# Attention: the product with V in fp32 in four column groups of 32

## The chip, the cores and the metric

The kernel runs on one core of one Trainium2 chip. The metric is the device time of an execution in microseconds. Its engines are TensorE (PE, with its weight loads as PEld), VectorE (DVE), ScalarE (ACT), GpSimd (POOL) and SyncE (SP, which here only starts DMAs). The matmul array can be used in parts: a matmul whose weights have 64 or fewer columns takes a column group, and two that use different groups can be on their way together.

## The reference

The program is one layer over 4096 tokens of width 256: a linear attention, a layer norm, then a transformer block (softmax attention with 16 heads of 16, and a mixture of 8 experts), and a last layer norm. The change touches the softmax attention alone:

```
h = _layernorm(x, ln1_g, ln1_b)
q = (h @ Wq).reshape(Bb, Ss, H, Dh)
k = (h @ Wk).reshape(Bb, Ss, H, Dh)
v = (h @ Wv).reshape(Bb, Ss, H, Dh)
scores = jnp.einsum('bqhd,bkhd->bhqk', q, k) / jnp.sqrt(jnp.float32(Dh))
attn = jax.nn.softmax(scores, axis=-1)
ctx = jnp.einsum('bhqk,bkhd->bqhd', attn, v).reshape(Bb, Ss, Dd)
```

Here Bb is 1, Ss is 4096, H is 16 and Dh is 16. All is fp32.

## The kernel before

The function `softmax_attention` goes through 128 chunks: 16 heads, each with 8 chunks of 512 queries. The 4096 keys stand on two sides of 2048, one in array rows 0 to 49 and one in rows 64 to 113, so that two score matmuls run beside each other. A chunk has 16 units t, each of 128 keys of either side. Each engine has its own program, and semaphores tie them together; the order on PE is written out by hand:

- In each slot t of a chunk PE computes the scores S of unit t (`scores`, two matmuls, line 701) into one of two banks `s_ps`, and ACT turns them into `probs` with Exp (line 790).
- Two chunks ahead (LEAD), PE computes the same products the other way round in pairs, M (`max_pair`, line 693), into three banks `m_ps` that take turns. DVE reduces each to a maximum over 512 keys (line 824, 683 ns). For the units in RELU_PAIRS, the first M holds a difference of two sides' keys, ACT takes its relu (line 777) and one DVE operation (line 818) adds the second M to it and reduces both at once. The next M into a bank waits (`m_read`, `excess_ready`) until the bank was read.
- In the slots of SLOTS, PE adds probabilities times V to `o_ps` (`values`, one or two units in a visit). Slots of 16 and more fall into the next chunk. Slot 9 and slot 11 have no visit.
- In slot 8 ACT copies `o_ps` to `o_here`, in slot 11 PE adds up its pieces through the matrix `gather` (`turn_o`, line 735), DVE copies the result to `ctx_stage` (line 832), and SP stores it.
- DVE's `finish_max` takes the maximum of a chunk in slot 0 and transposes it in slot 6 (line 842). Between the two POOL splits it in two parts (`split_max`, lines 628 to 631). SP writes it with 16 small DMAs (`rows`, line 545) as two more rows of the queries. PE waits for these before the chunk.

For 11 of the 16 units the product with V is split: the upper half of each fp32 probability read as bf16 and the rest of it as f16 (`probs_low`, which POOL computes, line 640), both against V in three bf16 pieces, 49 of 64 columns (line 726). The five FULL_UNITS take fp32 probabilities against fp32 V (line 720); these visits stand in slots 12, 15, 18, 21 and 24, that is in slots 12, 15, 2, 5 and 8 of a chunk. The last column of V is ones, which gives the sum of the probabilities. At the start of a head POOL splits V anew (`split_v`, lines 609 to 620).

Of the kernel before, what the change touches and what calls it, by code (L numbers as in the profile page):

```python
# [465 lines left out]
def softmax_attention(nc, dram, keep):  # L466

    with ExitStack() as ctx:
# [53 lines left out]
        def _(sp):  # L522
# [36 lines left out]
            def chunk(h, qc, loads=True, more=True, ahead=True, before=True):  # L559

                i = sp.snap(h * CHUNKS + qc)
                if loads:
                    sp.wait_ge(s_done, i * UNITS + 1)
                    n = qc + LEAD + 1
                    load_q(sp.snap(h + n // CHUNKS), n % CHUNKS, n % Q_BUFS)
                    if more and qc == 0:
                        load_head(sp.snap(h + 1), sp.snap((h + 1) & 1))
                if ahead:
                    rows(i + 1, (qc + 1) % Q_BUFS)
                if before:  # L570
# [14 lines left out]
        def _(pool):
            ch = Chain(pool, v_chain)
            nc.gpsimd.memset(k_ring[:, :, :].bitcast(F32), 1.0).then_inc(ones_set, 1)  # L587
            nc.gpsimd.memset(v_parts[:, :, :, V_ONE:V_COLS], 0.0).then_inc(v_consts, 1)
            nc.gpsimd.memset(v_full[:, :, :, :, :], 0.0).then_inc(v_consts, 1)
            nc.gpsimd.memset(zeros[:, :, :], 0.0).then_inc(v_consts, 1)  # L590
            nc.gpsimd.memset(gather[:, :], 0.0).then_inc(v_consts, 1)
            pool.wait_ge(v_consts, 4)
            nc.gpsimd.memset(v_parts[:, :, :, V_ONE:V_ONE + 1], 1.0).then_inc(v_consts, 1)
            nc.gpsimd.memset(v_full[:, :, :, :, V_ONE:V_ONE + 1], 1.0).then_inc(v_consts, 1)
            starts = [k * V_COLS + DH * n for k in range(2) for n in range(PIECES)]
            nc.gpsimd.tensor_tensor(gather[:, 0:DH], ident[:, 0:DH], ident[:, DH:2 * DH], ALU.add).then_inc(gather_chain, 1)
            for n, r in enumerate(starts[2:]):
                pool.wait_ge(gather_chain, n + 1)
                nc.gpsimd.tensor_tensor(gather[:, 0:DH], gather[:, 0:DH], ident[:, r:r + DH], ALU.add).then_inc(gather_chain, 1)
            nc.gpsimd.tensor_tensor(gather[:, DH:O_COLS], ident[:, V_ONE:V_ONE + 1],  # L600
                                    ident[:, V_COLS + V_ONE:V_COLS + V_ONE + 1], ALU.add).then_inc(gather_chain, 1)
            pool.wait_ge(gather_chain, len(starts))
            pool.wait_ge(v_consts, 6)
            pool.sem_inc(gather_ready, 1)

            def split_v(h, par):

                high, mid, low = (v_parts[:, par, :, DH * n:DH * n + DH] for n in range(PIECES))
                ch.inc(nc.gpsimd.tensor_copy(v_here[:, :, :], v_all[:, :, ds(h * DH, DH)]))
                ch.wait()  # L610
                for n, t in enumerate(FULL_UNITS):
                    at = first_tile(t)
                    ch.inc(nc.gpsimd.tensor_tensor(v_full[:, par, n, :, 0:DH], v_here[:, at:at + 3:2, :], zeros[:, 0:2, :], ALU.add))
                ch.inc(nc.gpsimd.tensor_tensor(high, v_here[:, :, :], zeros[:, :, :], ALU.add))
                ch.wait()
                ch.inc(nc.gpsimd.tensor_tensor(v_rest[:, :, :], v_here[:, :, :], high, ALU.subtract))
                ch.wait()
                ch.inc(nc.gpsimd.tensor_tensor(mid, v_rest[:, :, :], zeros[:, :, :], ALU.add))
                ch.wait()
                ch.inc(nc.gpsimd.tensor_tensor(low, v_rest[:, :, :], mid, ALU.subtract))  # L620
                ch.wait()
                pool.sem_inc(v_ready, 1)
# [11 lines left out]
            def split_probs(i, more=True):  # L634

                for t in POOL_UNITS:
                    if more and t == POOL_UNITS[MAX_PLACE]:
                        split_max(i + 1)
                    pool.wait_ge(exp_done, i * UNITS + (t + 1))
                    nc.gpsimd.tensor_tensor(probs_low[:, LOW_UNITS.index(t), :, :], probs[:, t, :, :],  # L640
                                            high_view[:, t, :, :, 1], ALU.subtract).then_inc(pool_low_done, 1)

            def split_chunks(lo, hi):
# [12 lines left out]
            split_chunks(0, CHUNKS + 1)  # L656
            with pool.Fori(0, HEADS // 2 - 1) as pair:
                ch.enter(pair, 2 * SPLIT_OPS)
                for par in range(2):
# [11 lines left out]
        def _(pe):
# [33 lines left out]
            def values(it, c, visit):  # L705
# [6 lines left out]
                for t in VISITS[visit]:  # L712
                    if t in POOL_UNITS:
                        pe.wait_ge(pool_low_done, i * len(POOL_UNITS) + (POOL_UNITS.index(t) + 1))
                    if t in DVE_UNITS:
                        pe.wait_ge(dve_low_done, i * (2 * len(DVE_UNITS)) + 2 * (DVE_UNITS.index(t) + 1))
                    first, final = t == VISITS[0][0], t == VISITS[-1][-1]
                    if t in FULL_UNITS:
                        for k in range(2):
                            last = nc.tensor.matmul(o_ps[V_COLS * k:V_COLS * k + V_COLS, :],  # L720
                                                    v_full[:, par, FULL_UNITS.index(t), k, :], probs[:, t, k, :],
                                                    start=False, stop=final)
                        continue
                    for n, part in enumerate((high_view[:, t, :, :, 1], probs_low[:, LOW_UNITS.index(t), :, :])):
                        for k in range(2):
                            last = nc.tensor.matmul(o_ps[V_COLS * k:V_COLS * k + V_COLS, :],  # L726
                                                    v_parts[:, par, first_tile(t) + 2 * k, :], part[:, k, :],
                                                    start=(first and n == 0), stop=(final and n == 1))
                last.then_inc(pv_done, 1)

            def turn_o(it, c):
# [3 lines left out]
                nc.tensor.matmul(m_ps[:, TURN_BLOCK % 3, :], gather[:, :], o_here[:, :], start=True, stop=True  # L735
                                 ).then_inc(o_turned, 1)
# [999 lines left out]
```

## Time and profile before

| what | us |
|---|---|
| median of 3 runs | 4357.15 |
| lowest and highest | 4355.73, 4363.25 |
| the profiled execution | 4349.05 |
| its span, first to last instruction | 4347.1 |
| attention's chunks in the span | about 357 to 3468 |
| PE, POOL, ACT, DVE busy | 3934.0, 3413.5, 2829.4, 2750.1 |
| mean granted clock of TensorE | 0.931 of full |

The page says how long each engine was busy. It does not say what waited for what: for that one reads the timeline of one chunk, engine by engine, and compares the start of an instruction with the end of what it needs. The records of one fp32 matmul are two, since it goes through the array in two passes; "x4" on line 720 stands for two matmuls.

### The profile page before, as it was taken

The page shows a single profiled execution, that of the slowest core. Times are in us where ns is not written, and L with a number is a line of the kernel's source. Part 1 is how long each engine was busy: PE and PEld are TensorE (multiplying, and loading weights), DVE is VectorE, ACT ScalarE, POOL GpSimd, SP SyncE. Part 2 cuts the span into 40 slices and gives each one's busy share as a digit, 9 for nine tenths or more (in the row PEclk, how much of TensorE's full clock was granted, in tenths as well). Part 3 has the DMA queues.
Part 4 walks back from the last instruction along what each step waited for, and adds up shares of the span by engine and source line. Part 5 has one row for each costly group of instructions (what it writes and reads, how often), then busy time and mean ns, then how long its engine had stood idle before and what let it go on. Part 6 is the DMA issues. An engine that isn't in the chain of part 4 may idle for free. (4 is left out here: it accounts for less than half of the span.)

```text
span 4347.1 us, 74722 instructions
## 1 busy us (share of the span) xinstructions
PE 3934.0 (90%) x21172; PEld 1901.6 (44%) x21172; DVE 2750.1 (63%) x5522; ACT 2829.4 (65%) x3421; POOL 3413.5 (79%) x2261
## 2 busy tenths in 40 slices
PE   7469999999999999999999999999999970999990
PEld 4234333333333333333333333333333360899990
DVE  2537777777777777777777777777777451333335
ACT  2125878777787878777787878777788710555550
POOL 0015898989888898988888898988988826888865
PEclk8677999999999999999999999999999975999995
DMA  2241011010101011010101011010100053443434
GB/s 86 111 137 19 11 21 22 10 22 10 22 10 22 10 22 21 11 21 10 22 10 22 10 22 21 11 21 12 20 11 10 17 186 109 140 144 132 147 101 121
DMA packets 145717, 205.12 MB, mean 47 GB/s; under 512 B 43536, under 2 KB 108432, under 8 KB 140176
## 3 DMA queue, kind: packets, MB, share of 16 engines
q1 hardware_dynamic: 127072, 173.76, 14.9%
q0 software_dynamic: 6336, 16.79, 1.2%
q10 hardware_dynamic: 12144, 12.06, 0.8%
q8 instruction: 141, 2.31, 0.2%
q14 instruction: 24, 0.20, 0.0%
HBM read 134.59 MB, written 66.85 MB: 46 GB/s over the span
## 5 line engine op out<-in xcount | busy, mean ns | idle before, releaser
L640 POOL TENSOR_TENSOR probs_low<-probs 128x1024 f16<-128x1024 f32 x1408 | 2632.3, 1894 | 331.0 <-ACT probs L790 324.6
L790 ACT ACTIVATE probs<-s_ps 128x1024 f32<-128x1024 f32 x2048 | 2081.7, 1026 | 240.3 <-PE s_ps L701 190.5
L824 DVE TENSOR_REDUCE unit_max<-m_ps 128x1 f32<-128x512 f32 x2816 | 1779.0, 683 | 222.4 <-PE m_ps L693 181.7
L701 PE MATMUL s_ps<-q_stage,k_ring 50*128 50x512 f32 x4096 | 1043.0, 504 | 1.2 <-DMA q_stage<-max_turned 0.9
L693 PE MATMUL m_ps<-k_ring,q_stage 48*128 48x512 f32 x3456 | 959.5, 424 | 64.3 <-DMA q_stage<-qs_dram 25.4
L701 PEld LDWEIGHTS s_ps<-q_stage,k_ring 50*128 50x128 f32 x4096 | 388.5, 186 | 1160.0 <-issue 907.8
L818 DVE CUSTOM_DVE_ANT_0 excess<-m_ps,excess 128x512 f32<-128x512 f32 x640 | 442.8, 692 | 550.5 <-ACT excess L777 543.9
L720 PE MATMUL o_ps<-probs,v_full 128*64 128x512 f32 x2560 | 698.0, 624 | 0.0
L777 ACT ACTIVATE excess<-m_ps 128x512 f32<-128x512 f32 x640 | 382.1, 597 | 449.8 <-PE m_ps L693 449.8
L726 PE MATMUL o_ps<-probs,v_parts 128*64 128x512 bf16 x2816 | 586.3, 413 | 0.9 <-POOL probs_low L640 0.7
L693 PEld LDWEIGHTS m_ps<-k_ring,q_stage 48*128 48x128 f32 x3456 | 514.8, 192 | 160.5 <-DVE unit_max L824 113.8
L726 PE MATMUL o_ps<-probs_low,v_parts 128*64 128x512 f16 x2816 | 543.2, 383 | 0.0
L1565 DVE TENSOR_TENSOR hidden_low<-h_ps,hidden_high 128x512 fp32r<-128x512 f32 x184 | 127.3, 692 | 365.7 <-ACT hidden_high L1529 365.7
L726 PEld LDWEIGHTS o_ps<-probs,v_parts 128*64 128x64 bf16 x2816 | 156.1, 108 | 379.0 <-issue 304.2
L1525 ACT ACTIVATE h_ps<-h_ps,b_here 128x512 f32<-128x512 f32 x184 | 121.3, 659 | 255.1 <-PE h_ps L1462 255.0
L693 PE MATMUL m_ps<-kd_ring,q_stage 48*128 48x512 f32 x640 | 258.3, 404 | 1.2 <-DVE unit_max L824 1.2
L587 POOL MEMSET k_ring<- 114x4096 f32 x1 | 3.5, 3516 | 293.0 <-POOLq L114 293.0
L1474 PE MATMUL y_ps<-w_low,hidden_high 128*128 128x256 f32 x736 | 209.0, 284 | 0.0
L1474 PE MATMUL y_ps<-w_high,hidden_high 128*128 128x256 f32 x736 | 207.4, 282 | 0.0
L1474 PE MATMUL y_ps<-w_high,hidden_low 128*128 128x256 f32 x736 | 206.6, 281 | 0.0
L720 PEld LDWEIGHTS o_ps<-probs,v_full 128*64 128x64 f32 x2560 | 127.6, 135 | 174.2 <-issue 173.6
L1421 POOL TENSOR_TENSOR w_high<-w_in,zero 128x1024 fp32r<-128x1024 f32 x44 | 130.5, 2983 | 68.3 <-PEq L1493 60.8
(198 smaller groups left out, 3586.6 us busy)
## 6 DMA issues: line engine op xcount, KB each, us to landing
w_in<-in_W SPq DMA_DIRECT2D x46, 1024.0 KB, 4.9
q_stage<-max_turned SPq DMA_DIRECT2D x2048, 0.5 KB
q_stage<-qs_dram SPq DMA_DIRECT2D x768, 32.0 KB, 1.8
k_ring<-ks_dram SPq DMA_DIRECT2D x96, 128.0 KB, 4.2
slots_dram<-zero_rows SPq DMA_DIRECT2D x24, 512.0 KB, 6.3
rows_e<-slots_dram SPq DMA_DIRECT2D x24, 512.0 KB, 3.9
y_slots_dram<-y_out ACTq DMA_DIRECT2D x23, 512.0 KB, 4.3
qs_dram<-parts SPq DMA_DIRECT2D x16, 512.0 KB, 2.8
```

Source lines behind the costliest of these rows:

```text
L640: nc.gpsimd.tensor_tensor(probs_low[:, LOW_UNITS.index(t), :, :], probs[:, t, :, :], high_view[:, t, :, :, 1], ALU.subtract).then_inc(pool ...
L693: nc.tensor.matmul(m_ps[:, b % 3, :], q_stage[at:at + SROWS, col:col + P], ring[at:at + SROWS, par, key:key + CHUNK], start=True, stop=Tru ...
L701: last = nc.tensor.matmul(s_ps[:, t % 2, k, :], k_ring[at:at + AROWS, par, P * t:P * t + P], q_stage[at:at + AROWS, buf * CHUNK:buf * CHUN ...
L720: last = nc.tensor.matmul(o_ps[V_COLS * k:V_COLS * k + V_COLS, :], v_full[:, par, FULL_UNITS.index(t), k, :], probs[:, t, k, :], start=Fal ...
L726: last = nc.tensor.matmul(o_ps[V_COLS * k:V_COLS * k + V_COLS, :], v_parts[:, par, first_tile(t) + 2 * k, :], part[:, k, :], start=(first ...
L777: nc.scalar.activation(excess[:, :], m_ps[:, block_of(t, 0) % 3, :], ACT.Relu).then_inc(excess_ready, 1)
L790: nc.scalar.activation(probs[:, t, :, :], s_ps[:, t % 2, :, :], ACT.Exp).then_inc(exp_done, 1)
L818: nc.vector.tensor_tensor_reduce(excess[:, :], m_ps[:, block_of(t, 1) % 3, :], excess[:, :], 1.0, LEAST, ALU.add, ALU.max, unit_max[:, b, ...
L824: nc.vector.tensor_reduce(unit_max[:, b, qt, 2 * j + k:2 * j + k + 1], m_ps[:, block_of(t, k) % 3, :], AX.X, ALU.max).then_inc(m_read, 1 + ...
L1421: nc.gpsimd.tensor_tensor(w1_high[:, b, half, :, :], w1[:, half, :, :], zero[:, :].unsqueeze(2).to_broadcast([P, FT, P]), ALU.add).then_in ...
L1474: last = nc.tensor.matmul(y_ps[:, b, t // 2, D * (t % 2):D * (t % 2) + D], h[:, f % 4, cols], w[:, b, f, :], start=(f == 0 and n == 0 and ...
L1565: nc.vector.tensor_tensor(hidden_low[:, f % 4, :], h_ps[:, f % 2, :], hidden_high[:, f % 4, :].bitcast(F32), ALU.subtract).then_inc(low_do ...
```

## The change

All 16 units now take fp32 probabilities against fp32 V. `probs_low`, the three pieces of V and all that POOL did for them are gone; POOL copies a head's V (`copy_v`) and splits the maxima. V has 32 columns for each key tile (16 values, a column of ones, zeros). A visit takes two units with their two sides, four matmuls in four column groups of 32, over half of the queries: a visit of all 512 queries in slot 10 for units 0 and 1, then 14 visits of 256 queries in slots 11 to 24. Only slot 9 has none. `turn_o` becomes four matmuls of 128 queries side by side, so that `ctx_stage` has 128 partitions by 128, and its store takes five DMAs in place of two. The relu units go from five (2, 5, 8, 12, 15) to four (2, 5, 11, 14), the transpose of the maxima from slot 6 to slot 2. Any M whose bank was last read by a relu now waits for ACT's signal. SP starts a head's K loads after the rows, not ahead of them.

```diff
-VISITS = ((0, 1), (3,), (2,), (4,), (6,), (5,), (7,), (9,), (8,), (10,), (12,), (11,), (13, 14), (15,))
-SLOTS = (10, 12, 13, 14, 15, 16, 17, 18, 19, 20, 21, 22, 23, 24)
+VISITS = ((0, 0, CHUNK),) + tuple((p, lo, lo + HALF) for p in range(1, UNITS // 2) for lo in (0, HALF))
+SLOTS = tuple(range(10, 25))
-RELU_PAIRS = (2, 5, 8, 12, 15)
-FINISH_SLOTS = (0, 6)
+RELU_PAIRS = (2, 5, 11, 14)
+FINISH_SLOTS = (0, 2)
...
-                    if more and qc == 0:
-                        load_head(sp.snap(h + 1), sp.snap((h + 1) & 1))
                 if ahead:
                     rows(i + 1, (qc + 1) % Q_BUFS)
+                if more and qc == 0:
+                    load_head(sp.snap(h + 1), sp.snap((h + 1) & 1))
...
+            def copy_v(h, par):
+
+                ch.inc(nc.gpsimd.tensor_copy(v_here[:, par, :, 0:DH], v_all[:, :, ds(h * DH, DH)]))
                 ch.wait()
                 pool.sem_inc(v_ready, 1)
...
-                    if k == 1 and (t - 1) % UNITS in RELU_PAIRS and t - 1 != TURN_SLOT and c * UNITS + t > 0:
+                    past = [r for r in RELU_PAIRS if block_of(r, 0) in (b - 3, b - 3 + RING_BLOCKS)]
+                    if past and c * RING_BLOCKS + b > 2:
...
+                pair, lo, hi = VISITS[visit]
+                for t in (2 * pair, 2 * pair + 1):
+                    for k in range(2):
+                        at = SQ * (2 * (t % 2) + k)
+                        last = nc.tensor.matmul(o_ps[at:at + SQ, lo:hi], v_here[:, par, first_tile(t) + 2 * k, :],
+                                                probs[:, t, k, lo:hi], start=(pair == 0), stop=(pair == UNITS // 2 - 1),
+                                                skip_group_check=True)
                 last.then_inc(pv_done, 1)
...
-                nc.tensor.matmul(m_ps[:, TURN_BLOCK % 3, :], gather[:, :], o_here[:, :], start=True, stop=True
-                                 ).then_inc(o_turned, 1)
+                for t in range(TPC):
+                    last = nc.tensor.matmul(m_ps[SQ * t:SQ * t + SQ, TURN_BLOCK % 3, 0:P], gather[:, :],
+                                            o_here[:, P * t:P * t + P], start=True, stop=True)
+                last.then_inc(o_turned, 1)
```

On PE, slots 2 and 3 and the start of slot 4 of a chunk, before (line 701 is S, 693 is M, 720 and 726 are V):

```order
L701 MATMUL s_ps<-q_stage,k_ring 128x512 [waits exp_done]
L701 MATMUL s_ps<-q_stage,k_ring 128x512
L693 MATMUL m_ps<-kd_ring,q_stage 128x512 [waits m_read]
L693 MATMUL m_ps<-k_ring,q_stage 128x512 [waits m_read]
L720 MATMUL o_ps<-probs,v_full 64x512 x2
L701 MATMUL s_ps<-q_stage,k_ring 128x512 [waits exp_done]
L701 MATMUL s_ps<-q_stage,k_ring 128x512
L693 MATMUL m_ps<-k_ring,q_stage 128x512 [waits m_read]
L693 MATMUL m_ps<-k_ring,q_stage 128x512 [waits excess_ready]
L726 MATMUL o_ps<-probs,v_parts 64x512 [waits pool_low_done]
L726 MATMUL o_ps<-probs,v_parts 64x512
L726 MATMUL o_ps<-probs_low,v_parts 64x512 x2
```

and in the changed kernel (line 661 is S, 653 is M, 676 is V):

```order
L661 MATMUL s_ps<-q_stage,k_ring 128x512 [waits exp_done]
L661 MATMUL s_ps<-q_stage,k_ring 128x512
L653 MATMUL m_ps<-kd_ring,q_stage 128x512 [waits m_read]
L653 MATMUL m_ps<-k_ring,q_stage 128x512 [waits m_read]
L676 MATMUL o_ps<-probs,v_here 32x256 x4
L661 MATMUL s_ps<-q_stage,k_ring 128x512 [waits exp_done]
L661 MATMUL s_ps<-q_stage,k_ring 128x512
L653 MATMUL m_ps<-k_ring,q_stage 128x512 [waits m_read]
L653 MATMUL m_ps<-k_ring,q_stage 128x512 [waits excess_ready]
L676 MATMUL o_ps<-probs,v_here 32x256 x4
L661 MATMUL s_ps<-q_stage,k_ring 128x512 [waits exp_done]
L661 MATMUL s_ps<-q_stage,k_ring 128x512
```

Behind the M pair of relu unit 2, two full matmuls of 512 queries have become four of 256, and the split visit of slot 3 another four.

On PE, slots 10 and 11, before:

```order
L701 MATMUL s_ps<-q_stage,k_ring 128x512 [waits exp_done]
L701 MATMUL s_ps<-q_stage,k_ring 128x512
L693 MATMUL m_ps<-k_ring,q_stage 128x512 [waits m_read] x2
L726 MATMUL o_ps<-probs,v_parts 64x512 [waits pool_low_done,o_copied]
L726 MATMUL o_ps<-probs,v_parts 64x512
L726 MATMUL o_ps<-probs_low,v_parts 64x512 x2
L726 MATMUL o_ps<-probs,v_parts 64x512 [waits pool_low_done]
L726 MATMUL o_ps<-probs,v_parts 64x512
L726 MATMUL o_ps<-probs_low,v_parts 64x512 x2
L701 MATMUL s_ps<-q_stage,k_ring 128x512 [waits exp_done]
L701 MATMUL s_ps<-q_stage,k_ring 128x512
L693 MATMUL m_ps<-k_ring,q_stage 128x512 [waits m_read] x2
```

and now, from S of slot 10 (line 686 is `turn_o`):

```order
L661 MATMUL s_ps<-q_stage,k_ring 128x512 [waits exp_done]
L661 MATMUL s_ps<-q_stage,k_ring 128x512
L653 MATMUL m_ps<-k_ring,q_stage 128x512 [waits m_read] x2
L676 MATMUL o_ps<-probs,v_here 32x512 [waits o_copied]
L676 MATMUL o_ps<-probs,v_here 32x512 x3
L661 MATMUL s_ps<-q_stage,k_ring 128x512 [waits exp_done]
L661 MATMUL s_ps<-q_stage,k_ring 128x512
L653 MATMUL m_ps<-kd_ring,q_stage 128x512 [waits m_read]
L653 MATMUL m_ps<-k_ring,q_stage 128x512 [waits m_read]
L676 MATMUL o_ps<-probs,v_here 32x256 x4
L686 MATMUL m_ps<-o_here,gather 32x128 [waits m_read,o_copied]
L686 MATMUL m_ps<-o_here,gather 32x128 x3
```

Slot 10 keeps a long visit, now of one pair of units; slot 11 has become a relu slot with a visit ahead of `turn_o`, which is four matmuls of 128 queries.

On SP, a head's first chunk, before (line 535 loads queries, 526 and 529 the next head's K, 545 writes rows):

```order
L535 DMA q_stage<-qs_dram 16x512 [waits s_done]
L535 DMA q_stage<-qs_dram 16x512 x5
L526 DMA k_ring<-ks_dram 16x2048 x6
L529 DMA kd_ring<-kd_dram 16x2048 x3
L545 DMA q_stage<-max_turned 1x4x32 [waits max_ready]
L545 DMA q_stage<-max_turned 1x4x32 x15
L535 DMA q_stage<-qs_dram 16x512 [waits s_done]
```

and now (518, 509 and 512, 528):

```order
L518 DMA q_stage<-qs_dram 16x512 [waits s_done]
L518 DMA q_stage<-qs_dram 16x512 x5
L528 DMA q_stage<-max_turned 1x4x32 [waits max_ready]
L528 DMA q_stage<-max_turned 1x4x32 x15
L509 DMA k_ring<-ks_dram 16x2048 x6
L512 DMA kd_ring<-kd_dram 16x2048 x3
L518 DMA q_stage<-qs_dram 16x512 [waits s_done]
```

The rows of the next chunk no longer stand behind the nine K loads.

## Rows read from the trace of the kernel before

**Rows 1.** The page: busy time of each engine over the span.

```profile
PE 3934.0 (90%) x21172; PEld 1901.6 (44%) x21172; DVE 2750.1 (63%) x5522; ACT 2829.4 (65%) x3421; POOL 3413.5 (79%) x2261
```

**Rows 2.** Busy time by stretch: us, engines with (instructions), PEclk, DMA share, GB/s.

```profile
400.00:3440.00 3040.00, 3003.02 (x16256) 1173.45 (x16252) 2250.82 (x4356) 2392.53 (x2752) 2721.79 (x1893) 0.98 0.09 16
769.00:798.00 29.00, 27.36 (x138) 10.56 (x134) 18.78 (x38) 19.93 (x24) 28.10 (x25) 0.88 0.04 9
```

**Rows 3.** Timeline, SyncE, 1400 to 1610 us: start, us, engine, line, operation.

```profile
1408.75 2.69 SPq L535 DMA_DIRECT2D q_stage<-qs_dram  x6
...
1551.06 2.69 SPq L535 DMA_DIRECT2D q_stage<-qs_dram  x6
...
1579.36 2.69 SPq L535 DMA_DIRECT2D q_stage<-qs_dram  x6
```

**Rows 4.** The same for PE, 1500 to 1526 us, one chunk's slots 6 to 12.

```profile
1511.33 0.50 PE L701 MATMUL s_ps<-q_stage,k_ring 50*128 50x512 f32 x2
...
1512.00 0.41 PE L726 MATMUL o_ps<-probs,v_parts 128*64 128x512 bf16 x2
...
1512.56 0.50 PE L701 MATMUL s_ps<-q_stage,k_ring 50*128 50x512 f32 x2
...
1514.62 0.40 PE L693 MATMUL m_ps<-kd_ring,q_stage 48*128 48x512 f32 x1
...
1514.94 1.08 PE L720 MATMUL o_ps<-probs,v_full 128*64 128x512 f32 x4
1515.95 0.50 PE L701 MATMUL s_ps<-q_stage,k_ring 50*128 50x512 f32 x2
1516.29 0.40 PE L693 MATMUL m_ps<-k_ring,q_stage 48*128 48x512 f32 x2
1516.62 0.49 PE L701 MATMUL s_ps<-q_stage,k_ring 50*128 50x512 f32 x2
1516.95 1.02 PE L693 MATMUL m_ps<-k_ring,q_stage 48*128 48x512 f32 x2
1517.90 0.42 PE L726 MATMUL o_ps<-probs,v_parts 128*64 128x512 bf16 x2
...
1519.57 1.13 PE L735 MATMUL m_ps<-o_here,gather 128*128 128x512 f32 x2
1520.63 0.50 PE L701 MATMUL s_ps<-q_stage,k_ring 50*128 50x512 f32 x2
```

**Rows 5.** The same for PE's weight loads, 1517 to 1518 us.

```profile
1517.47 0.18 PEld L693 LDWEIGHTS m_ps<-k_ring,q_stage 48*128 48x128 f32 x1 [0.56 <-DVE unit_max L824]
```

**Rows 6.** The same for ACT.

```profile
1515.05 0.60 ACT L777 ACTIVATE excess<-m_ps 128x512 f32<-128x512 f32 x1 [0.85 <-PE m_ps L693]
```

**Rows 7.** The same for DVE.

```profile
1513.31 0.23 DVE L842 STREAM_TRANSPOSE max_turned<-max_parts 128x64 f32<-128x64 f32 x1
1513.47 1.25 DVE L824 TENSOR_REDUCE unit_max<-m_ps 128x1 f32<-128x512 f32 x2
1515.92 0.69 DVE L818 CUSTOM_DVE_ANT_0 excess<-m_ps,excess 128x512 f32<-128x512 f32 x1 [1.20 <-ACT excess L777]
...
1516.73 2.48 DVE L824 TENSOR_REDUCE unit_max<-m_ps 128x1 f32<-128x512 f32 x4
```

**Rows 8.** All engines at the start of a head, 769 to 785 us.

```profile
769.74 0.61 POOL L609 COPY v_here<-v_all 128x512 f32 x1
...
781.37 0.24 DVE L842 STREAM_TRANSPOSE max_turned<-max_parts 128x64 f32<-128x64 f32 x1 [2.38 <-POOL max_parts L631]
```

**Rows 9.** SyncE in a head's first chunk.

```profile
1333.06 3.00 SPq L526 DMA_DIRECT2D k_ring<-ks_dram  x6
1336.26 1.34 SPq L529 DMA_DIRECT2D kd_ring<-kd_dram  x3
1339.94 9.87 SPq L545 DMA_DIRECT2D q_stage<-max_turned  x16
```

**Rows 10.** Busy time of line 1116 alone, the densest stretch of loads and matmuls.

```profile
3535.40:3537.00 1.60, 1.60 (x15) 1.60 (x16) 1.00 1.04 339
```

More of the change, by code:

```diff
@@ L84, in visit_of @@
 def visit_of(t):
-    return [t in units for units in VISITS].index(True)
+    return max(n for n, (pair, lo, hi) in enumerate(VISITS) if pair == t // 2)
 class Chain:
@@ L593, in _ @@
[L593 to L603, printed above, removed]
-            pool.sem_inc(gather_ready, 1)
[L606 to L620, printed above, removed]
@@ new lines, in _ @@
+            pool.wait_ge(v_consts, 2)
+            nc.gpsimd.memset(v_here[:, :, :, DH:O_COLS], 1.0).then_inc(v_consts, 1)
+            nc.gpsimd.tensor_tensor(gather[:, 0:O_COLS], ident[:, 0:O_COLS], ident[:, SQ:SQ + O_COLS], ALU.add
+                                    ).then_inc(gather_chain, 1)
+            for n in range(2, P // SQ):
+                pool.wait_ge(gather_chain, n - 1)
+                nc.gpsimd.tensor_tensor(gather[:, 0:O_COLS], gather[:, 0:O_COLS], ident[:, SQ * n:SQ * n + O_COLS], ALU.add
+                                        ).then_inc(gather_chain, 1)
@@ L632, in split_max, with split_maxima @@
                                         ).then_inc(max_split, 1)
[L634 to L643, printed above, removed]
+            def split_maxima(lo, hi):
                 with pool.Fori(lo, hi) as i:
-                    split_probs(i)
+                    split_max(i + 1)
             for h in range(2):
-                split_v(h, h)
+                copy_v(h, h)
             pool.wait_ge(unit_set, 3)
@@ L655, in _ @@
                                     ).then_inc(max_split, 1)
-            split_chunks(0, CHUNKS + 1)
+            split_maxima(0, CHUNKS + 1)
             with pool.Fori(0, HEADS // 2 - 1) as pair:
-                ch.enter(pair, 2 * SPLIT_OPS)
+                ch.enter(pair, 2)
                 for par in range(2):
@@ L711, in values @@
                     pe.wait_ge(v_ready, it * 2 + (c // CHUNKS + 1))
[L712 to L728, printed above, removed]
+                pair, lo, hi = VISITS[visit]
[5 more added lines that the diff above has]
+                                                skip_group_check=True)
                 last.then_inc(pv_done, 1)
@@ L843, in finish_max, with chunk @@
                                         max_parts[:, :, :].bitcast(F32).rearrange("p r n -> p (r n)")).then_inc(max_ready, 1)
-            def low(i, t, k):
-                dve.wait_ge(exp_done, i * UNITS + (t + 1))
-                nc.vector.tensor_tensor(probs_low[:, LOW_UNITS.index(t), k, :], probs[:, t, k, :], high_view[:, t, k, :, 1],
-                                        ALU.subtract).then_inc(dve_low_done, 1)
-            def chunk(n, b, ahead=True, finish=True, turn=True, stores=None, current=True):
+            def chunk(n, b, ahead=True, finish=True, turn=True, stores=None):
                 for t in range(UNITS):
@@ L863, in chunk @@
                             dve.sem_inc(m_read, RING_BLOCKS - 1 - TURN_BLOCK)
-                    if current and t in DVE_PLACES:
-                        low(n - LEAD, *DVE_PLACES[t])
                     if finish and not ahead and t == FINISH_SLOTS[0]:
@@ L869, in chunk @@
                         finish_max(n - 1, 1 - b, FINISH_SLOTS.index(t))
-            chunk(0, 0, finish=False, turn=False, current=False)
-            chunk(1, 1, turn=False, current=False)
+            chunk(0, 0, finish=False, turn=False)
+            chunk(1, 1, turn=False)
             chunk(2, 0, turn=False)
@@ L881, in _ @@
             chunk(RING + 1, 1, ahead=False, finish=False, stores=RING // 2 - 1)
-            chunk(RING + 2, 0, ahead=False, finish=False, stores=RING // 2 - 1, current=False)
+            chunk(RING + 2, 0, ahead=False, finish=False, stores=RING // 2 - 1)
 def row_statistics(nc, dve, ch, stats, mean_var, std, rstd, var_ready, std_ready, n):
```

53 lines of the change are left out of this document (18 added, 35 removed).

## The prediction

> **What bounds the kernel now.** I read the page first, then the busy time by stretch. Over the span PE is busy 90%, POOL 79%, ACT 65%, DVE 63% [rows 1]. In the attention stage, 400 to 3440 us, PE is busy 3003 of 3040 us, POOL 2722, and the granted clock is 0.98, so nearly all of it at the upper of the two levels, 2.4 GHz [rows 2]. The reader is to see that the stage is 70% of the span and that PE has no room in it; the other stages are untouched by the diff and stay as they are.
>
> Next, the period of a chunk from SyncE's query loads: six chunks start between 1408.75 and 1551.06, 23.72 us each, and the seventh, the second of a head, takes 28.30 [rows 3]. There are 128 chunks and 14 such long ones, 4.58 us each above the others.
>
> Then one chunk on PE in order of time [rows 4]. A slot is a score pair S, a maximum pair M, and mostly a visit of the values, V. S to M is 0.34 us (1515.95 to 1516.29), M to what follows 0.33 (1516.29 to 1516.62). A split unit (bf16 and f16) takes 0.56 (1512.00 to 1512.56), a full fp32 unit 1.01 (1514.94 to 1515.95), turn_o 1.06 (1519.57 to 1520.63). Added up for a chunk: 16 x 0.67 + 11 x 0.50 (four of the split units stand in two visits of about 1.0, so 7 x 0.56 + 2 x 1.0 = 5.9) + 5 x 1.01 + 1.06 = 22.7 us. The other 1.0 us of 23.72 is waiting, and one place holds most of it: at slot 10 the second M waits from 1516.95 to 1517.47 and V starts at 1517.90 in place of 1517.28, 0.62 late [rows 4, 5].
>
> Last, why it waits, since the change rearranges just that. A relu unit runs PE, ACT, DVE in series: M starts at 1514.62, relu at 1515.05, the DVE operation at 1515.92, the next reduce at 1516.73, and the M two units later goes at 1517.47, when that reduce has freed its bank [rows 4 to 7]. So from M to relu 0.43, to DVE 0.87, to the next reduce 0.81, to the freed bank 0.74: 2.85 us. PE needs two slots for that way, and where they are shorter it waits. Before, a full unit of 1.01 us stands behind the M of each relu unit, and only the empty slot 9 is too short.
>
> **The change part by part.**
>
> *Values.* 54 matmuls in 14 visits become 60 in 15: one of 512 queries, 14 of 256, each with four matmuls in four column groups. The trace has only two groups at once. Full minus split unit is 1.01 - 0.56 = 0.45 us; both have two groups, and the full one streams twice as long, so 0.43 to 0.45 us is what half the columns of a full visit take. If four groups stream beside each other as two do, a half visit takes 1.01 - 0.43 = 0.58 us and holds two units. Bounds: 0.56 (a split visit, which streams as long), and 1.01 if the groups go two by two. I take 0.58, the nearest row. The sum is 14 x 0.58 + 1.01 = 9.1 us a chunk against 10.9.
>
> *turn_o.* One fp32 matmul of 512 columns becomes four of 128 side by side: about 0.4 us in place of 1.06 (a quarter of the 0.86 that streams, and the 0.2 around it). Its output on DVE shrinks too. Neither ends up on the path, see the walk.
>
> PE without any wait would then need 16 x 0.67 + 9.1 + 0.4 = 20.3 us a chunk, 2.4 less than the 22.7 of before. That would be 2.4 x 127 = 305 us plus the saved waits. I do not take it, because the slots behind relu units are now 1.25 us each (0.34 + 0.33 + 0.58), 2.5 for two, and the way across ACT and DVE takes 2.85 and its wait breaks up an M pair.
>
> *The walk of one chunk, with relu at units 2, 5, 11, 14.* Times from S of slot 2.
> - Relu 2: M 0.34, relu 0.77, DVE 1.64, free 2.45, the transpose that now stands here 0.16 (1513.31 to 1513.47) [rows 7], reduce of unit 3 at 2.61, bank free 3.35. M of unit 4 would have been at 2.84, so it waits 0.5. A lone second M takes 0.43 to V (1517.47 to 1517.90). V 0.58, S of slot 5 at 4.36. The banks that a relu frees are now waited for by ACT's own signal, which comes before DVE's and is on time.
> - Relu 5: 2.45 + 0.74 + 0.43 + 0.58 = 4.20, S of slot 8 at 8.56; slot 8 nothing special, S of slot 9 at 9.81.
> - Slot 9 is empty: its reduce starts 0.77 after S, bank free 1.51, then 0.43, and V of 512 queries 1.01: S of slot 11 at 12.76.
> - Relu 11: M of unit 12 waits for the DVE operation itself, free at 2.37; + 0.43 + 0.58: S of slot 13 at 16.14. turn_o (0.4) ends before that wait does and costs nothing.
> - Slot 13 1.25, relu 14 4.20: S of slot 1 at 21.59, slot 1 1.25, S of slot 2 at 22.84.
>
> So the period is 22.84 us, not 20.3: DVE and the relu way become the bound and PE waits 2.5 us a chunk. The gain is 23.72 - 22.84 = 0.88 us x 127 = 112 us. A V that is off by 0.05 counts seven times on this path, 0.35 us.
>
> *POOL.* It loses all low parts (79% busy falls to a few per cent). They cost PE little in an ordinary chunk, but at a head's start the split of V (from 769.74) holds POOL up and DVE waits 2.38 us for the maxima behind it at 781.37, PE behind DVE; the clock there averages 0.88 [rows 2, 8]. What remains is one copy of V, 0.61 us. So the 14 long chunks become ordinary: 14 x 4.58 = 64 us. What is late next there is SyncE: nothing of PE waits for the K loads until the next head.
>
> *SyncE.* In a head's first chunk: query loads 2.7, rows 9.87, K loads 3.00 + 1.34, and five stores in place of two, about 2.5: 19.4 us against 22.8 [rows 3, 9]. The rows now go ahead of the K loads: they start behind the transpose of slot 2, about 5 us into the chunk, and are all issued by about 15. Cost nothing; if the cover is gone, 1 to 4 us in 15 chunks. The wait of a store holds only the next query loads, which are wanted two chunks later.
>
> *Rest.* relu 4 for 5, with two more reduces, is in the walk. The end of the stage has no POOL wait and shorter visits, but three more stores: about -1.
>
> Sum against the profiled execution's 4349 us: 4349 - 112 - 64 - 1 = 4172. The median of the runs, 4357, is 8 us above that execution; I forecast 4174.
>
> **The rivals.**
>
> 1. *Column groups two by two.* A half visit takes 1.01, the long one 1.87, turn_o 0.7: 10.7 + 14.1 + 1.9 + 0.7 = 27.4, with a wait left at slot 10 about 27.6 us. (27.6 - 23.72) x 127 = +493, - 64: 4777. It decides from a half visit of 0.78 on: the period is then 22.84 + 7 x 0.20 = 24.2, whose loss of 0.5 us a chunk eats the heads' 64 us. For it: no row shows more than two groups, and four read four different fp32 streams at once. Against: the two that run now show no slowing by each other. 0.11.
> 2. *Four groups at once but dearer*, 0.65 to 0.75 a half visit, by the streams or by issue. A load with its matmul comes every 0.107 us at the densest [rows 10]; a slot now has 12 such pairs, 1.28 us against its 1.25. At 0.70: 22.84 + 7 x 0.12 = 23.7, only the heads' 64 us are gained: 4285. 0.08. The Trainium skill ("TensorE: Matmul & The Clock Gate", section Measured speedup) gives 2.38x for three column tiles and 3.07x for four row tiles, not 3 and 4. By an estimate from 3.07 of 4 a half visit would be 0.71 and the time that of this rival; no run here shows four groups.
> 3. *PE does not wait*: the way across ACT and DVE overlaps better than my walk has it, period 21.5 or less: 4349 - 282 - 65 = 4000. Against: the 0.62 at slot 10 comes out of the same steps. 0.05.
> 4. *The clock.* PE's idle share grows from about 4% to 11%. After the 2.4 us wait at a head's start it fell [rows 2, 8]; the longest wait of the walk is 0.5. If chunks ran at 1.2 GHz, S, M and V double: over 30 us a chunk, above 5000. 0.03.
>
> **How the numbers follow.** The walk has 0.73, with a range of its own of 22.2 to 23.4 us a chunk, 4090 to 4245. The range is 4085 to 4265: it adds the mild end of rival 2 and leaves out 0.11 for rival 1, 0.03 for the clock, and about 0.07 beyond the rest. What a measurement of this kernel can tell from no change is 0.2%, 9 us. Faster: 0.73 + 0.05 + most of rival 2 = 0.84. Same 0.03. Slower 0.13, rivals 1 and 4 with one case of rival 2 beyond the even point.
>
> **What would show it.** From one half visit's start to the next S: 0.58 (right), 0.7 (rival 2), 1.01 (rival 1). Query loads 22.8 us apart, the head's second chunk like the others. Second M of units 4, 7, 10, 12 and 0 waiting for DVE 0.3 to 0.5 us each, and the relu way still 0.43, 0.87, 0.81, 0.74. No POOL wait, clock 0.98 or more. Wrong would be: PE full at 20.3 us, waits at other units, or a wait of DVE for rows or stores.

## The result, and the profile after

The changed kernel takes 4080.6 us (median of 4 runs, 4078.6 to 4083.5), the kernel before on the same chip 4356.4 us (4353.6 to 4363.3): a ratio of 0.9365, 95% interval 0.9349 to 0.9381. It is 276 us faster; the forecast was 182 us faster, 4174 us, with a range from 4085 to 4265. The measured time lies 4 us below that range.

The page of the changed kernel, busy time of each engine over its span of 4078.9 us, beside [rows 1]:

```profile
PE 3651.7 (90%) x29108; PEld 1882.1 (46%) x29108; DVE 2718.8 (67%) x5522; ACT 2680.2 (66%) x3293; POOL 696.5 (17%) x703
```

and the attention stage by stretch, the columns those of [rows 2]:

```profile
400.00:3200.00 2800.00, 2745.12 (x24272) 1161.52 (x24264) 2220.80 (x4357) 2267.46 (x2655) 77.07 (x389) 1.00 0.10 18
```

POOL has lost its work, PE stays at the same share of a shorter stage, and the granted clock is 1.00, the upper level, 2.4 GHz. SyncE's query loads from a head's first chunk on stand beside [rows 3]; they are 22.10, 21.53 and 22.15 us apart:

```profile
1248.93 2.70 SPq L518 DMA_DIRECT2D q_stage<-qs_dram  x6
...
1271.03 2.70 SPq L518 DMA_DIRECT2D q_stage<-qs_dram  x6
...
1292.56 2.70 SPq L518 DMA_DIRECT2D q_stage<-qs_dram  x6
...
1314.71 2.70 SPq L518 DMA_DIRECT2D q_stage<-qs_dram  x6
```

There is no chunk of 28 us any more. Measured from one chunk's first exponential to the next one's, the median period is 23.72 us before and 22.15 us after. So the time went like this in the two profiled executions, which are 268 us apart (4349.1 and 4080.7): 1.57 us x 127 periods = 199 us; the 14 long chunks were 74 us above 23.72 in all (eight of them 4.6, three 6.1, one 7.7, one 9.1, one 2.1) and are gone; the end of the stage gave 2 to 3. The attention stage is 276 us shorter, from the start of the first exponential to the end of the last. Around it 8 us were lost again, 1 ahead of it and 7 behind, and nothing points to the change there: the time behind the attention stage lay between 881 and 896 us over all ten profiled executions of this study (886.5 before, 893.1 after), in no order with what was changed.

Then PE through one chunk (columns as in [rows 4]; line 661 is S, 653 M, 676 V, 686 `turn_o`). First the piece without a wait, then relu unit 2 (slot at 1693.34) and the next two:

```profile
1690.04 0.64 PE L676 MATMUL o_ps<-probs,v_here 128*32 128x256 f32 x8
1690.61 0.50 PE L661 MATMUL s_ps<-q_stage,k_ring 50*128 50x512 f32 x2
...
1693.34 0.50 PE L661 MATMUL s_ps<-q_stage,k_ring 50*128 50x512 f32 x2
1693.68 0.39 PE L653 MATMUL m_ps<-kd_ring,q_stage 48*128 48x512 f32 x1
...
1694.94 0.39 PE L653 MATMUL m_ps<-k_ring,q_stage 48*128 48x512 f32 x2
...
1696.17 0.78 PE L653 MATMUL m_ps<-k_ring,q_stage 48*128 48x512 f32 x2
1696.88 0.64 PE L676 MATMUL o_ps<-probs,v_here 128*32 128x256 f32 x8
1697.45 0.51 PE L661 MATMUL s_ps<-q_stage,k_ring 50*128 50x512 f32 x2
...
1701.44 0.50 PE L661 MATMUL s_ps<-q_stage,k_ring 50*128 50x512 f32 x2
...
1705.62 0.50 PE L661 MATMUL s_ps<-q_stage,k_ring 50*128 50x512 f32 x2
...
1706.74 0.40 PE L686 MATMUL m_ps<-o_here,gather 128*32 128x128 f32 x8
1707.08 0.50 PE L661 MATMUL s_ps<-q_stage,k_ring 50*128 50x512 f32 x2
```

A half visit takes 1690.61 - 1690.04 = 0.57 us: four streams of 256 columns beside each other. `turn_o` takes 0.34. The M pair of unit 4 takes 0.78 where an unhindered one takes 0.39: its second matmul waits for its weights, and this weight load waits for DVE to free the bank. The weight loads of unit 4 and of unit 12:

```profile
1696.45 0.18 PEld L653 LDWEIGHTS m_ps<-k_ring,q_stage 48*128 48x128 f32 x1 [0.32 <-DVE unit_max L776]
...
1708.02 0.18 PEld L653 LDWEIGHTS m_ps<-k_ring,q_stage 48*128 48x128 f32 x1 [0.65 <-DVE unit_max L770]
```

and the relu way, for unit 2 on ACT, for units 2 and 5 on DVE:

```profile
1694.10 0.60 ACT L729 ACTIVATE excess<-m_ps 128x512 f32<-128x512 f32 x1 [0.44 <-PE m_ps L653]
```

```profile
1694.97 0.69 DVE L770 CUSTOM_DVE_ANT_0 excess<-m_ps,excess 128x512 f32<-128x512 f32 x1 [0.81 <-ACT excess L729]
...
1695.58 0.24 DVE L794 STREAM_TRANSPOSE max_turned<-max_parts 128x64 f32<-128x64 f32 x1
1695.75 2.45 DVE L776 TENSOR_REDUCE unit_max<-m_ps 128x1 f32<-128x512 f32 x4
1699.08 0.69 DVE L770 CUSTOM_DVE_ANT_0 excess<-m_ps,excess 128x512 f32<-128x512 f32 x1 [0.89 <-ACT excess L729]
...
1699.70 6.23 DVE L776 TENSOR_REDUCE unit_max<-m_ps 128x1 f32<-128x512 f32 x10
```

M to relu is 1694.10 - 1693.68 = 0.42, relu to DVE 0.87, both as before. But the handover, from the start of DVE's relu operation to the start of what DVE does next, is 0.61 and 0.62 us, not the 0.81 of [rows 7]. Against the walk of the prediction the steps of this chunk, from S to S, are:

| step | forecast | measured |
|---|---|---|
| slot 2 to 5 | 4.36 | 4.11 |
| slot 5 to 8 | 4.20 | 3.99 |
| slot 8 to 9 | 1.25 | 1.23 |
| slot 9 to 11 (the long visit) | 2.95 | 2.95 |
| slot 11 to 13 | 3.38 | 3.39 |
| slot 13 to 14 | 1.25 | 1.23 |
| slot 14 to 1 | 4.20 | 4.00 |
| slot 1 to 2 | 1.25 | 1.24 |
| sum | 22.84 | 22.14 |

The waits that delay PE are where the walk put them and nowhere else. The three steps with relu units 2, 5 and 14 are each 0.20 to 0.25 shorter than forecast.

### The profile page after: what moved, and what is told of

It reads as the page before. It is cut to its first block and busy times, and to the rows that moved or that the text cites. A ratio compares the mean times of both kernels' runs of the same rounds, so it can differ in the third digit from the quotient of the medians.

```text
span 4078.9 us, 88141 instructions
## 1 busy us (share of the span) xinstructions
PE 3651.7 (90%) x29108; PEld 1882.1 (46%) x29108; DVE 2718.8 (67%) x5522; ACT 2680.2 (66%) x3293; POOL 696.5 (17%) x703
## 5 line engine op out<-in xcount | busy, mean ns | idle before, releaser
L776 DVE TENSOR_REDUCE unit_max<-m_ps 128x1 f32<-128x512 f32 x3072 | 1917.4, 681 | 79.8 <-PE m_ps L653 75.8
L676 PE MATMUL o_ps<-probs,v_here 128*32 128x256 f32 (+1 forms) x15360 | 1282.9, 406 | 0.5 <-ACT probs L742 0.5
L653 PE MATMUL m_ps<-k_ring,q_stage 48*128 48x512 f32 x3584 | 1106.5, 428 | 71.7 <-DVE unit_max L770 26.2
L770 DVE CUSTOM_DVE_ANT_0 excess<-m_ps,excess 128x512 f32<-128x512 f32 x512 | 354.2, 692 | 490.9 <-ACT excess L729 489.6
L676 PEld LDWEIGHTS o_ps<-probs,v_here 128*32 128x32 f32 x15360 | 303.1, 108 | 547.9 <-issue 544.9
L1406 PE MATMUL h_ps<-m_high,w_high 128*128 128x512 f32 x368 | 150.4, 409 | 4.7 <-issue 4.2
L1406 PE MATMUL h_ps<-m_high,w_low 128*128 128x512 f32 x368 | 145.6, 396 | 0.0
L1406 PE MATMUL h_ps<-m_low,w_high 128*128 128x512 f32 x368 | 145.1, 394 | 0.0
L1418 PEld LDWEIGHTS y_ps<-w_high,hidden_high 128*128 128x128 f32 x736 | 138.0, 188 | 7.9
L1418 PEld LDWEIGHTS y_ps<-w_low,hidden_high 128*128 128x128 f32 x736 | 138.1, 188 | 7.4
```

Of the source, the lines that this page charges most:

```text
L653: nc.tensor.matmul(m_ps[:, b % 3, :], q_stage[at:at + SROWS, col:col + P], ring[at:at + SROWS, par, key:key + CHUNK], start=True, stop=Tru ...
L676: last = nc.tensor.matmul(o_ps[at:at + SQ, lo:hi], v_here[:, par, first_tile(t) + 2 * k, :], probs[:, t, k, lo:hi], start=(pair == 0), sto ...
L770: nc.vector.tensor_tensor_reduce(excess[:, :], m_ps[:, block_of(t, 1) % 3, :], excess[:, :], 1.0, LEAST, ALU.add, ALU.max, unit_max[:, b, ...
L776: nc.vector.tensor_reduce(unit_max[:, b, qt, 2 * j + k:2 * j + k + 1], m_ps[:, block_of(t, k) % 3, :], AX.X, ALU.max).then_inc(m_read, 1 + ...
L1406: last = nc.tensor.matmul(h_ps[:, f % 2, :], w[:, b, half, f, :], m[:, b, half, :], start=(half == 0 and n == 0), stop=(half == HALVES - 1 ...
L1418: last = nc.tensor.matmul(y_ps[:, b, t // 2, D * (t % 2):D * (t % 2) + D], h[:, f % 4, cols], w[:, b, f, :], start=(f == 0 and n == 0 and ...
```

## The experiments

Two theories stood for those 0.2 us. *Way*: DVE was never slower before; its next reduce at 1516.73 [rows 7] waited for the M pair that PE ran from 1516.29 for 0.40 us [rows 4], so 0.81 was PE's time in the row of another engine. *Contention*: POOL, busy 90% of the attention stage before [rows 2], shares something with DVE and lengthens the handover, 0.81 with POOL busy, 0.62 with POOL idle.

**e1_pool_busy**: the changed kernel with ten idle operations of the old size on POOL in each chunk, on buffers of their own.

```diff
...
+            def busy(i):
+                for n in range(BUSY_OPS):
+                    pool.wait_ge(idle_done, i * BUSY_OPS + (n + 1))
+                    nc.gpsimd.tensor_tensor(idle_out[:, :], idle_in[:, :], idle_in[:, :], ALU.subtract).then_inc(idle_done, 1)
...
```

> The changed kernel, with ten subtractions of 128x1024 fp32 into f16 added on POOL behind each chunk's split of the maxima, of buffers that nothing else uses; no engine waits for them. Theory (POOL's work delays DVE behind the relu operation): in the changed kernel the instruction behind the relu operation starts 0.62 us after it, before it was 0.81 in the attention loop and 0.62 in the lead-in, where POOL was idle. With POOL busy it is 0.81 again at most relu units, three of the four lie on the path, the chunk takes 22.6 to 22.9 us in place of 22.15 and the kernel 4140 to 4175. Rival (the 0.19 us come from the program, for example from the place of the transpose or from the relu units' places): 0.62 stays, 22.15 and 4080 stay.

Measured: 4075.9 us, 0.9369 (0.9353 to 0.9385) of before, as the changed kernel. Its busy time by stretch, POOL the fifth engine, and then POOL's and DVE's timeline at one relu unit:

```profile
400.00:3160.00 2760.00, 2715.76 (x23940) 1150.63 (x23938) 2215.27 (x4347) 2238.36 (x2619) 2430.21 (x1636) 1.00 0.10 18
```

```profile
1688.21 9.78 POOL L611 TENSOR_TENSOR idle_out<-idle_in 128x1024 f16<-128x1024 f32 x5
```

```profile
1693.70 0.69 DVE L782 CUSTOM_DVE_ANT_0 excess<-m_ps,excess 128x512 f32<-128x512 f32 x1 [0.90 <-ACT excess L741]
...
1694.31 3.80 DVE L788 TENSOR_REDUCE unit_max<-m_ps 128x1 f32<-128x512 f32 x6
```

The handover is 1694.31 - 1693.70 = 0.61 with POOL busy throughout (2430 of the 2760 us shown), and the period stays 22.15. Contention falls. The Trainium skill ("SBUF — State Buffer", section Who interferes with whom) has it so: a DVE instruction with at most one SBUF input, outside the 2-port modes, does not contend with GpSimd; DVE's relu operation reads one tile of SBUF and one of PSUM. e6 below settles it from the other side: there POOL is mostly idle, and the handover is 0.81.

**e2_no_relu**: does the relu way hold PE?

```diff
-RELU_PAIRS = (2, 5, 11, 14)
+RELU_PAIRS = ()
```

> The changed kernel with no relu units: DVE reduces all 32 maximum blocks of a chunk, ACT has four operations less. Theory (the way PE, ACT, DVE of a relu unit sets the period, with PE's waits behind each): DVE needs 32 x 0.60 + 0.6 = 19.8 us, PE 20.3 without a wait, and a chunk takes 20.5 to 21.0 us, the kernel 3870 to 3940. Rival (DVE's load as such bounds the chunk, of which relu units take off 2 x 0.60 - 0.62 us each): eight reduces more make it as long or longer, 22.15 to 22.8, 4080 to 4160.

Measured: 3960.6 us, 0.9100 (0.9083 to 0.9118), period 21.17 us. Without the relu way it is 115 us below e1, which ran beside it on the same chip, although DVE then does two reduces in place of one operation in four units and is busy 2527.4 of 2640 us (400 to 3040 us). So the relu way did hold PE. The size was not met: the period is 0.17 us and the time 21 us above what was expected. Two waits are left: behind `turn_o`, and at the second M of slot 10, behind the slot without a visit:

```profile
1691.29 0.40 PE L686 MATMUL m_ps<-o_here,gather 128*32 128x128 f32 x8
1691.62 0.51 PE L661 MATMUL s_ps<-q_stage,k_ring 50*128 50x512 f32 x2
1691.96 0.81 PE L653 MATMUL m_ps<-k_ring,q_stage 48*128 48x512 f32 x2
...
1709.92 0.50 PE L653 MATMUL m_ps<-k_ring,q_stage 48*128 48x512 f32 x1 [0.17 <-DVE unit_max L776]
1710.35 1.07 PE L676 MATMUL o_ps<-probs,v_here 128*32 128x512 f32 x8
```

**e3_full_visits_no_relu**: e2 with eight visits of 512 queries, one every second slot, to have fewer switches between V and the others.

```diff
-VISITS = ((0, 0, CHUNK),) + tuple((p, lo, lo + HALF) for p in range(1, UNITS // 2) for lo in (0, HALF))
-SLOTS = tuple(range(10, 25))
+VISITS = tuple((p, 0, CHUNK) for p in range(UNITS // 2))
+SLOTS = tuple(range(10, 25, 2))
```

> As the one without relu units, and the values in eight visits of 512 queries in slots 10, 12, ..., 24 in place of one of 512 and 14 of 256. Each visit has about 0.15 us that does not stream, so PE saves 7 x 0.15 = 1.0 us a chunk and needs 19.2 without a wait. Theory: DVE (19.8) then bounds, with PE waiting in the short slots: 19.8 to 20.3 us a chunk, 3780 to 3850 us. Rival (the even spread of the visits is what keeps DVE fed, two slots of 1.68 and 0.67 us break it): 20.8 to 21.5, slower than the one with halves.

Measured: 4324.3 us, 0.9936 (0.992 to 0.9953), period 24.11. Neither expectation held. PE, two slots long:

```profile
1700.79 1.06 PE L676 MATMUL o_ps<-probs,v_here 128*32 128x512 f32 x8
1701.79 0.49 PE L661 MATMUL s_ps<-q_stage,k_ring 50*128 50x512 f32 x2
1702.12 0.40 PE L653 MATMUL m_ps<-k_ring,q_stage 48*128 48x512 f32 x2
1702.36 0.40 PE L661 MATMUL s_ps<-q_stage,k_ring 50*128 50x512 f32 x2
1702.60 0.40 PE L653 MATMUL m_ps<-k_ring,q_stage 48*128 48x512 f32 x1
1703.30 0.49 PE L653 MATMUL m_ps<-k_ring,q_stage 48*128 48x512 f32 x1 [0.31 <-DVE unit_max L776]
1703.72 1.07 PE L676 MATMUL o_ps<-probs,v_here 128*32 128x512 f32 x8
```

Two slots take 2.93 us (1700.79 to 1703.72), eight times that is 23.4 of the 24.11. There are three maximum banks. A slot without a visit lets the next M pair come 0.48 us behind the last (1702.12 to 1702.60), its first matmul takes the third bank, and its second needs the first of them back, which DVE frees only at 1703.30: M to reduce 0.44, reduce to freed bank 0.74. DVE then has nothing to do during the long visit (its waits for M sum to 472.5 us between 400 and 3400). So the halves of 256 queries matter too, 364 us between e3 and e2: V in every slot keeps the slots equal, 1.23 us, which is just what DVE needs for two reduces (four in 2.45 us, at 1695.75 above).

**e4_before_max_first**: the kernel before with only the order of POOL's work changed: the chunk's maxima ahead of all its low parts, where two of them stood ahead. The split of V, at a head's start, still stands ahead of both.

```diff
-MAX_PLACE = 2
+MAX_PLACE = 0
```

> The kernel before with one number changed: POOL splits the maxima ahead of the first low part of a chunk (MAX_PLACE 0), not ahead of the third. Theory (a head's second chunk is long because DVE waits for the maxima behind POOL's split of V, and PE behind DVE, until its clock falls): the two low parts of 3.8 us no longer stand between, the wait of 2.4 us at the transpose goes, the long chunks shrink from 28.3 us to 25 to 26.5, and the kernel gains 25 to 45 us. Rival (PE waits for the low parts that come 6.8 us late, whatever the order): 28.3 and 4356 stay.

Measured: 4284.3 us, 0.9852 (0.9835 to 0.9868), period 23.72 unchanged and no long chunk left. Its query loads from the second chunk of the head of [rows 9] on; in the kernel before this chunk took 31.40 us:

```profile
1333.01 2.69 SPq L535 DMA_DIRECT2D q_stage<-qs_dram  x6
...
1356.74 2.69 SPq L535 DMA_DIRECT2D q_stage<-qs_dram  x6
...
1380.46 2.69 SPq L535 DMA_DIRECT2D q_stage<-qs_dram  x6
```

and POOL's maxima in that chunk:

```profile
1340.87 0.20 POOL L628 TENSOR_TENSOR neg_max<-no_max,tile_max 128x4 f32<-128x4 f32 x1 [0.46 <-POOL v_parts L620]
```

They still come right behind the split of V (`v_parts`, line 620). What is gone are the two low parts between, 3.75 us, and with them DVE's wait at the transpose, which in the kernel before was 2.37 us in this chunk: between 400 and 3160 us the trace of e4 has no wait of DVE for POOL. The gain is 68 us, against the 25 to 45 expected. So the split of V alone costs PE nothing; the long chunks came from the split together with the two low parts behind it, and one number of the old kernel was worth a quarter of the change.

**e5_k_loads_first**: the changed kernel with the K loads ahead of the rows on SyncE again.

```diff
-                if ahead:
-                    rows(i + 1, (qc + 1) % Q_BUFS)
                 if more and qc == 0:
                     load_head(sp.snap(h + 1), sp.snap((h + 1) & 1))
+                if ahead:
+                    rows(i + 1, (qc + 1) % Q_BUFS)
```

> The changed kernel with SyncE's K loads ahead of the rows again, as before the change. Theory (the prediction's: this part is worth nothing, the rows have time): no change, 22.15 us a chunk everywhere, 4075 to 4083. Rival (moving the rows ahead took part in shortening a head's start): the first chunk of each head is 1 to 4 us longer, 4095 to 4140.

Measured: 4075.9 us (4068.7 to 4087.8), 0.9382 (0.935 to 0.9415), period 22.15, no long head chunk: the order is worth nothing, as forecast. The spread of 19 us is told below.

**e6_two_groups**: the kernel before, with 15 of the 16 units in full fp32 in its two column groups, and the maxima first.

```diff
-FULL_UNITS = (3, 6, 9, 12, 15)
+FULL_UNITS = tuple(range(1, 16))
...
-MAX_PLACE = 2
+MAX_PLACE = 0
```

> The kernel before with fifteen of its sixteen units in full fp32 (one unit stays split, MAX_PLACE is 0): the values in fp32 without the four column groups. PE: 16 x 0.67 + 0.56 + 15 x 1.01 + 1.06 = 27.5 us a chunk less the joint visits' 0.3. Theory (the four groups stream side by side and carry the change, POOL's relief is the smaller part): 27.2 to 27.9 us a chunk, 4750 to 4850 us. Rival (POOL was what held the kernel before): about 23.7 or less in spite of the longer visits.

Measured: 4814.9 us, 1.1086 (1.1049 to 1.1122), period 27.93. PE, and DVE at a relu unit:

```profile
1705.20 1.08 PE L720 MATMUL o_ps<-probs,v_full 128*64 128x512 f32 x4
1706.21 0.50 PE L701 MATMUL s_ps<-q_stage,k_ring 50*128 50x512 f32 x2
1706.56 0.40 PE L693 MATMUL m_ps<-k_ring,q_stage 48*128 48x512 f32 x2
```

```profile
1706.18 0.69 DVE L818 CUSTOM_DVE_ANT_0 excess<-m_ps,excess 128x512 f32<-128x512 f32 x1 [1.26 <-ACT excess L777]
...
1706.99 1.29 DVE L824 TENSOR_REDUCE unit_max<-m_ps 128x1 f32<-128x512 f32 x2
```

Full fp32 in two groups costs 1.01 us a unit and makes the kernel 11% slower; in four groups two units together take the same 1.00 us (e3, 1700.79 to 1701.79). The four groups carry the change: without them the time is near that of rival 1, 4777.

The DVE rows also settle the 0.2 us. POOL is busy 340.2 of 2760 us here, and from the relu operation to the next reduce are 1706.99 - 1706.18 = 0.81 us all the same. The reduce starts 0.43 behind the M pair that it reads (1706.56). Behind every relu operation between 400 and 3000 us, 548 in e4's trace and 465 in e6's, the reduce starts 0.42 to 0.44 us behind an M pair, whether the handover is 0.80 or 1.03; in the kernel before it is so outside the long chunks. *Way* holds.

**e7_no_relu_turn10** and **e8_relu10_turn10**: what e2 points to. `turn_o` goes behind the long visit of slot 10, which gives DVE the time to free the banks; e8 adds one relu unit there, so that its way is covered by that visit.

```diff
-COPY_SLOT, TURN_SLOT = 8, 11
-RELU_PAIRS = (2, 5, 11, 14)
+COPY_SLOT, TURN_SLOT = 8, 10
+RELU_PAIRS = ()
```

> The changed kernel without relu units, and turn_o in slot 10, behind the long visit, in place of slot 11. Theory (three banks in turn: the block of turn_o takes one of them, so that M of the next slot waits for the first reduce of its own slot's predecessor; in slot 10 the long visit covers this): the wait of 0.42 us in slot 12 goes and none comes in slot 11, 20.75 us a chunk for 21.17, 3905 to 3915 us against 3960. Rival (DVE's reduces, 19.8 us with its small work, are the bound and the wait only moves): 21.1 to 21.2, 3955 to 3965.

> As that one, with one relu unit, 10, whose way through ACT and DVE (2.4 us to the freed bank behind it) lies beside the long visit and turn_o. Theory: where the slots behind are long enough a relu unit costs PE nothing and takes 0.58 us off DVE: 20.6 to 20.8 us a chunk, equal to or 20 us below the one without. Rival (every relu unit costs its 0.2 to 0.4): 21.0 to 21.2.

Measured: e7 3901.1 us, 0.8981 (0.8958 to 0.9003), period 20.79; e8 (`RELU_PAIRS = (10,)`) 3903.7 us, 0.8999 (0.8968 to 0.903), period 20.78. Both beat both kernels and are 4.3% below e5, the changed kernel but for one order on SyncE, on the same chip; between them there is no difference beyond the noise. e7's PE around the long visit, and what its weight loads wait for from 400 to 2990 us (us in total, times, longest):

```profile
1708.24 0.49 PE L653 MATMUL m_ps<-k_ring,q_stage 48*128 48x512 f32 x1 [0.18 <-DVE unit_max L776]
1708.66 1.07 PE L676 MATMUL o_ps<-probs,v_here 128*32 128x512 f32 x8
1709.54 0.40 PE L686 MATMUL m_ps<-o_here,gather 128*32 128x128 f32 x8
1709.87 0.50 PE L661 MATMUL s_ps<-q_stage,k_ring 50*128 50x512 f32 x2
```

```profile
PEld m_ps L653 <- DVE unit_max L776: 89.0, 248, 0.5
```

`turn_o` now costs 0.33 us and no wait. The two loads of slot 10 are the only ones that wait for DVE in a chunk (248 waits in 125 chunks, 0.7 us a chunk). From 400 to 2990 us DVE is busy 2535.9 of 2590 us and PE 2568.4: a further step would have to relieve both.

## Why the prediction was right, and where it was not

**Direction and mechanism: right, the size outside the range.** Half visits take 0.57 us (0.58 forecast), the long one 1.00 (1.01), the waits stand at units 4, 7, 10, 12 and 0, one wait for POOL in the whole stage (0.7 us), SyncE's order free (e5), clock 1.00. Rivals 1 and 2 fell with the half visit, rival 4 with the clock, rival 3 with the period: 22.15 is above its 21.5, and the relu way does hold PE (e2). But it named the direction of the miss: the way is shorter than the walk has it.

**The step that failed** is one term of the walk: "to the next reduce 0.81". I read it off [rows 7] as a time of DVE's. The row ahead of it on PE shows otherwise: the next M pair had started at 1516.29 and taken 0.40, so its data came at 1516.69 and the reduce began at 1516.73 [rows 4, 7]. The 0.81 held PE's time of the slot before, which the change shortens. DVE's own handover is 0.62, in the changed kernel and in e1. The relu way is 0.43 + 0.87 + 0.62 + 0.74 = 2.66 us, not 2.85. The term stood in three steps of the walk: 3 x 0.19 = 0.57 us a chunk, 72 us in all; with 0.62 in its place the same sum gives 4100. The rest of the 0.69 us between 22.84 and 22.15 are the visits' 0.01 each and 0.04 at unit 4, where reduce to freed bank took 0.70 (1695.75 to 1696.45) and not 0.74. 0.69 x 127 = 88 us. The sum of the prediction missed the profiled execution by 4172 - 4080.7 = 91: these 88, 10 of the heads and 1 to 2 of the stage's end, less the 8 lost around the stage.

The mistake was a row read as a duration where it was a wait. It went unmarked in that row, since DVE was idle there for 0.12 us only and the row names no releaser. Where the same handover was longer the profile of the kernel before did mark it, at 1357.98 us with 0.18 us of waiting for M. The range shared it: its low end, 22.2 us a chunk, is above the 22.15 measured.

**The heads' term**, 64 us, was right in kind and 10 us short: I took the typical 4.58 for all 14 chunks, and five of them were 6.1 to 9.1 longer. The granted clock tells these apart. Around a chunk of 28.3 us it is 0.88 [rows 2], around the one of 31.4 us 0.79, around the one of 32.9 us 0.74, and the one of 25.8 us kept 1.00:

```profile
1353.00:1386.00 33.00, 31.36 (x144) 11.74 (x142) 19.80 (x39) 20.87 (x24) 28.69 (x25) 0.79 0.04 8
```

By an estimate from these (a PE that is always busy loses the missing share of the clock) 0.12 x 29 = 3.5 of the 4.6 us are time at the lower clock, and 0.21 x 33 = 6.9 of the 7.7. The chunk that kept its clock was 2.1 us longer. So what makes a long chunk as long as it is, and one longer than another, is for the most part the time at 1.2 GHz behind the wait. The sum is right that the wait behind POOL causes it: e4 has neither the wait nor any of these chunks, and its granted clock from 400 to 3380 us is 1.00. But the prediction puts the wait behind the split of V alone, and e4 shows that the two low parts were needed for it.

## What to carry to other kernels

A gap between two rows of one engine is that engine's time only if its next input was already there: look up when the input ended before the gap goes into a sum, above all where the change moves that input. When a change makes the bounding engine's work shorter and more even, read the way across the other engines (here M, relu, DVE, freed bank: 2.66 us, where two slots are 2 x 1.23) and put what is long behind what is long, or drop it: that was worth another 175 us here (e5 to e7). And try the order on a helper engine first: moving the maxima ahead on POOL was worth 68 us with one number.

## What the runs showed of the hardware

- Four column groups of 32, each with fp32 weights of 128 x 32 and its own stream, run beside each other without slowing: 256 columns of four in 0.57 us, 512 of four in 1.00, 512 of two groups of 64 in 1.01 (e6), and 512 of a single matmul over all 128 columns in 1.06 (`turn_o` before, [rows 4]). From 256 to 512 columns adds 0.43 us; by an estimate from this, 0.14 us of a half visit does not grow with its columns. The Trainium skill ("TensorE: Matmul & The Clock Gate", Measured speedup) has 2.38x for three column tiles and 3.07x for four row tiles; by the prediction's estimate from it a half visit would be 0.71 us. The measurement decides: nothing of that loss shows here.
- The first chunk of the stage runs at the lower clock, and when the clock rises differs from run to run. By stretch, e5's first two chunks and the third:

```profile
358.00:385.00 27.00, 26.84 (x115) 12.45 (x112) 19.02 (x38) 18.05 (x20) 0.55 (x3) 0.50 0.35 52
385.00:421.00 36.00, 36.00 (x196) 12.18 (x196) 18.88 (x36) 18.83 (x21) 0.55 (x3) 0.50 0.04 7
421.00:445.00 24.00, 23.70 (x210) 9.88 (x212) 19.32 (x39) 19.28 (x23) 0.55 (x3) 0.98 0.06 14
```

  The second chunk is at 1.2 GHz, PE without a gap, and takes 35.3 us. In the changed kernel's profile it runs at 1.00 and takes 21.8, 13 us less. The edit does not explain this, since e5's own four runs differ as much: 4068.7 and 4068.9 us with a mean granted clock of 0.942, 4082.8 and 4087.8 with 0.936 and 0.935. The trace is that of the run of 4082.8; that the second chunk is the whole of the distance is not shown.
